# Attention denominators by way of HBM instead of 0/1 products on TensorE

## The reference

```
x = x + attention(layernorm(x))     # 16 heads of 16 channels, rotary q and k, ALiBi bias, softmax
x = x + layernorm(x) @ (W + C V_r).T + b
```

## Time and profile before

| | |
|---|---|
| median of three runs | 2109.35 us (2106.3 to 2109.4) |
| the profiled execution | span 2108.7 us; no time beyond its span is listed for it |
| PE busy | 2074.9 us, 98% |
| DVE busy | 1855.8 us, 88% |
| ACT busy | 1513.9 us, 72% |
| POOL busy | 1296.4 us, 61% |
| time from one batch to the next | 62.7 us (1038.66 to 1101.38 for the first product of the spread, in the chain that ended last) |
| mean TensorE clock granted | 0.989 of full speed |

### The profile page before, as it was taken

One profiled execution on the slowest core, in us unless ns is written; L12 is line 12 of the kernel. 1 busy time (PEld: TensorE's weight loads), 2 busy tenths in 40 slices (PEclk: granted clock), 3 DMA queues, 4 the chain that ended last, 5 costly groups with the idle time before them and its releaser, 6 DMA issues.

```text
span 2108.7 us, 81949 instructions
## 1 busy us (share of the span) xinstructions
PE 2074.9 (98%) x33596; PEld 1193.3 (57%) x33596; DVE 1855.8 (88%) x5459; ACT 1513.9 (72%) x2562; POOL 1296.4 (61%) x1093
## 2 busy tenths in 40 slices
PE   6999999999999999999999999999999999999998
PEld 3455555555555555555555555555555555555554
DVE  7899998988998998999898999998999999999972
ACT  2377777777777777787777777777777777777664
POOL 6357566667565667666666666666766666766512
PEclk8699999999999999999999999999999999999999
DMA  5343333433333433334333334334333334333311
GB/s 156 92 115 102 87 112 105 112 116 104 94 103 107 114 113 105 96 101 124 94 113 109 100 97 121 104 105 123 101 86 115 104 109 121 102 95 104 97 51 39
DMA packets 158935, 218.78 MB, mean 104 GB/s; under 512 B 19072, under 2 KB 104960, under 8 KB 158560
## 3 DMA queue, kind: packets, MB, share of 16 engines
q1 hardware_dynamic: 157280, 211.44, 35.5%
q10 hardware_dynamic: 1280, 2.10, 0.3%
HBM read 36.52 MB, written 16.78 MB: 25 GB/s over the span
## 4 chain that ended last, share of the span: by engine, by line
PE 91%; DVE 1%; ACT 1%; issue 1%; POOL 0%; DVEq 0%
PE ps_s L436 30%; PE ps_o L459 21%; PE ps_misc L413 18%; PE ps_misc L400 12%; PE ps_misc L387 3%; PE ps_misc L478 3%; PE ps_t L446 2%; PE ps_misc L469 2%; DVE junk L648 1%; ACT pt L840 0%; PE ps_t L519 0%; ACT x_res L788 0%; ACT x_res L783 0%; DVE x_hat L684 0%; DVE x_res L633 0%
## 5 line engine op out<-in xcount | busy, mean ns | idle before, releaser
L648 DVE CUSTOM_DVE_ANT_0 junk<-ps_s,alibi 128x512 bf16<-128x512 f32 x2004 | 1302.7, 687 | 185.7 <-PE ps_s L436 153.6
L840 ACT ACTIVATE pt<-ps_t 128x1024 f32<-128x1024 f32 x1024 | 1049.6, 1025 | 450.5 <-DVE ps_t L661 441.4
L446 PE MATMUL ps_t<-at 64*128 64x512 f32 x2048 | 762.2, 451 | 2.3 <-ACT pt L840 2.0
L436 PE MATMUL ps_s<-at 64*128 64x512 f32 x2004 | 757.7, 454 | 3.6 <-DVE row_max L648 2.8
L459 PE MATMUL ps_o<-pt,v_one 128*17 128x128 f32 x16384 | 637.4, 273 | 1.4 <-ACT pt L840 1.3
L459 PEld LDWEIGHTS ps_o<-pt,v_one 128*17 128x17 f32 x16384 | 441.1, 98 | 184.2 <-issue 46.0
L436 PEld LDWEIGHTS ps_s<-at 64*128 64x128 f32 x2004 | 325.6, 184 | 240.9 <-DVE row_max L648 133.4
L661 DVE TENSOR_TENSOR ps_t<-ps_t,diag 128x256 f32<-128x256 f32 x1024 | 435.5, 425 | 14.5 <-PE ps_t L446 14.4
L1006 POOL TENSOR_TENSOR rope_b<-raw,rope_sin 128x512 f32<-128x512 f32 x128 | 164.5, 1285 | 327.3 <-ACT raw L820 323.6
L1022 POOL TENSOR_TENSOR halves<-rope_a,swapped 128x512 fp32r<-128x512 f32 x126 | 159.3, 1287 | 322.8 <-DMA swapped<-rope_b 322.8
L446 PEld LDWEIGHTS ps_t<-at 64*128 64x128 f32 x2048 | 328.1, 184 | 13.9 <-ACT pt L840 8.7
(11 more groups left out here) (105 smaller groups left out, 1801.0 us busy)
## 6 DMA issues: line engine op xcount, KB each, us to landing
at<-halves SPq DMA_DIRECT2D x192, 512.0 KB, 4.0
swapped<-rope_b SPq DMA_DIRECT2D x256, 128.0 KB, 2.6
x_in<-in_L_attn_x_dram SPq DMA_DIRECT2D x32, 512.0 KB, 5.2
num<-o_sb SPq DMA_DIRECT2D x512, 32.0 KB
x_res<-in_L_attn_x_dram SPq DMA_DIRECT2D x32, 512.0 KB, 4.3
out_dram<-x_hat SPq DMA_DIRECT2D x32, 512.0 KB, 5.8
at<-spread_den SPq DMA_DIRECT2D x60, 64.0 KB
at<-max_t ACTq DMA_DIRECT2D x128, 16.0 KB
```

Of the source, the lines that this page charges most:

```text
L436: pe.matmul(scores_bank(n, t), operand(n, 0)[:, t * P:(t + 1) * P], operand(n, 1), start=True, stop=True).then_inc(s_done, 1)
L446: pe.matmul(ps_t[:, j, :], operand(n, 1)[:, j * P:(j + 1) * P], operand(n, 0), start=True, stop=True).then_inc(t_done, 1)
L648: dve.tensor_tensor_reduce(unused, scores_bank(n, t), alibi[:, off:off + N], 1.0, LOWEST, ALU.add, ALU.max, row_max[:, hb % 2, t, hh:hh + ...
L840: act.activation(pt[:, h % 2, 2 * pair:2 * pair + 2, :], ps_t[:, 2 * pair:2 * pair + 2, :], ACT.Exp).then_inc(exp_done, 1)
```

## The change

The denominators of a batch are written to an array in HBM (`den_dram`) instead of the tile. At slot 29 SP waits for the four writes and loads them back as 128 rows of 64. DVE takes one reciprocal of 128 x 64 in half-slot 32 b + 59. At slot 30 SP waits for it and writes the result to HBM (`recip_dram`). At slot 31 SP waits for that write and issues four loads that repeat each head's row over 16 partitions, into the new tile `spread`. DVE multiplies `spread` by `num` in half-slots 64 and 65, one later than before. The 64 products of a batch on PE and their table are gone. The zeros for `clear_max` move from the table's free rows to free rows of the tile that holds the turned maxima.

```diff
-XT, DEN, X2T = (-26, -25), (63, 64), (79, 80)
+XT, X2T = (-26, -25), (79, 80)
+GATHER_SLOT, RECIPROCAL_SLOT, PARK_SLOT, SPREAD_SLOT = 29, 29, 30, 31
+DIVIDE = (64, 65)
...
-        den = sb("den", [P, P])
+        den = sb("den", [P, HALF])
+        spread = sb("spread", [P, KC, N])
...
+        den_dram = nc.dram_tensor("den_dram", (NB, H, N), F32).ap()
+        recip_dram = nc.dram_tensor("recip_dram", (NB, H, N), F32).ap()
...
-            def denominators(b, half):
-
-                if half == 0:
-                    dve.wait_ge(den_placed, 16 * G * (b + 1))
-                mine = slice(half * HALF, (half + 1) * HALF)
-                dve.reciprocal(den[0:T * H, mine], den[0:T * H, mine]).then_inc(den_done, 1)
+            def denominators(b):
+
+                dve.wait_ge(den_gathered, 16 * (b + 1))
+                dve.reciprocal(den[:, :], den[:, :]).then_inc(den_done, 1)
...
             def divide(b, kc):
-                dve.wait_ge(misc_full, full_at["den", b, kc])
                 if kc == 0:
                     dve.wait_ge(num_placed, 16 * T * G * (b + 1))
+                    dve.wait_ge(spread_placed, 16 * G * (b + 1))
                     if b:
                         dve.wait_ge(x1_done, 2 * b)
-                dve.tensor_tensor(attn_t[:, kc, :], bank_at("den", b, kc), num[:, kc, :], ALU.mult).then_inc(attn_done, 1)
+                dve.tensor_tensor(attn_t[:, kc, :], spread[:, kc, :], num[:, kc, :], ALU.mult).then_inc(attn_done, 1)
...
+            def gather_denominators(b):
+
+                sp.wait_ge(den_placed, 16 * G * (b + 1))
+                if b:
+                    sp.wait_ge(recip_parked, 16 * b)
+                sp.dma_start(den[:, :], den_dram[b].rearrange("h (t q) -> (h t) q", q=HALF)).then_inc(den_gathered, 16)
+
+            def park_reciprocals(b):
+
+                sp.wait_ge(den_done, b + 1)
+                sp.dma_start(recip_dram[b].rearrange("h (t q) -> (h t) q", q=HALF), den[:, :]).then_inc(recip_parked, 16)
+
+            def spread_denominators(b):
+
+                sp.wait_ge(recip_parked, 16 * (b + 1))
+                if b:
+                    sp.wait_ge(attn_done, KC * b)
+                for g in range(G):
+                    src = recip_dram[b, HG * g:HG * (g + 1), :].rearrange("(o i) q -> o i q", o=1).broadcast_to([D, HG, N])
+                    sp.dma_start(spread[(g % 2) * HALF:(g % 2 + 1) * HALF, g // 2, :], src).then_inc(spread_placed, 16)
...
-                    sp.dma_start(den[g * T * HG:(g + 1) * T * HG, :], o_sb[D::32, :, :]).then_inc(den_placed, 16)
+                    dst = den_dram[b, HG * g:HG * (g + 1), :].rearrange("i (t q) -> t i q", t=T)
+                    sp.dma_start(dst, o_sb[D::32, :, :]).then_inc(den_placed, 16)
```

More of the change, by code:

```diff
@@ L98, in shape_constants @@
     of_head = of_head.reshape(P, -1)
[L101 to L108, removed]
+    return {"rope_cos": rows(cos, cos), "rope_sin": rows(sin, -sin), "before": before, "diag": diag,
             "qpat": np.concatenate([qpat, qpat], 0), "kpat": spread(kpat).astype(f), "pick": np.concatenate([spread(pick), of_head], 1).astype(f), "ident": np.eye(P, dtype=f)}
@@ L161, in layer @@
         max2 = sb("max2", [P, T, 2 * 8])
-        max_t = sb("max_t", [2 * 8, N], F32R)
+        turned = sb("turned", [P, N], F32R)
+        max_t = turned[0:2 * 8, :]
+        no_max = turned[HALF:HALF + M_ROWS, :].bitcast(F32)
         junk = sb("junk", [P, 2, N], mybir.dt.bfloat16)
@@ L289, in bank_of @@
                 return "misc"
-            return {"den": "s0", "proj": "s1", "x2t": "s0", "ffn": "s1"}.get(kind, "misc")
+            return {"proj": "s1", "x2t": "s0", "ffn": "s1"}.get(kind, "misc")
         def bank_at(kind, b, u):
@@ L470, in max_rows @@
                 misc_filled(ins, ("max", hb), max_turned, hb + 1)
[L472 to L481, removed]
             def turn_weights():
@@ L576, in tensor_program @@
                             turn_tokens("x2t", b, kc, x_hat2, xhat_done2, b + 1 + (b == NB - 1), x2t_done)
-                        b, quarters = due(now, DEN[kc])
-                        if b is not None:
-                            spread_denominators(b, kc)
                     if hb is not None and half == 1:
@@ L685, in add_linear @@
                                   other[:, two, :], ALU.add).then_inc(done, 1)
-            dve.memset(spread_den[T * H:P, :, :, :], 0.0)
-            dve.memset(den[T * H:P, :], 0.0)
+            dve.memset(no_max, 0.0)
             dve.memset(alibi[:, 0:U_W // 2], 0.0).then_inc(cleared, 1)
@@ L735, in vector_program @@
                         slope_block(2 * (n - 3) + half)
-                    for part in range(2):
-                        b = batch_at(slot, (29, 30)[part])
-                        if b is not None and half == 1 - part:
-                            denominators(b, part)
+                    b = batch_at(slot, RECIPROCAL_SLOT)
+                    if b is not None and half == 1:
+                        denominators(b)
                     now = 2 * slot + half
                     for kc in range(KC):
-                        b = complete_at(now, DEN[kc])
+                        b = complete_at(now, DIVIDE[kc])
                         if b is not None:
@@ L1109, in sync_program @@
                                      o_sb[32 * t:32 * t + D, :, :]).then_inc(num_placed, 16)
+                b = batch_at(slot, GATHER_SLOT)
+                if b is not None:
+                    gather_denominators(b)
+                b = batch_at(slot, PARK_SLOT)
+                if b is not None:
+                    park_reciprocals(b)
+                b = batch_at(slot, SPREAD_SLOT)
+                if b is not None:
+                    spread_denominators(b)
                 hb = half_at(slot, -8)
```

4 lines of the change are left out of this document (1 added, 3 removed).

## The result

The changed kernel takes **2336.26 us** in the median of four runs (2329.26 to 2346.06), against 2109.18 of the kernel before beside it: a ratio of 1.108 (1.105 to 1.112). The forecast was 2227, with a range that ended at 2300. The direction and the stall came out, but the kernel lost 227 us where 118 were forecast. The profiled execution has a span of 2339.0 us and a mean clock of 0.947, where before had 2108.7 and 0.989.

The account below looks back on a forecast made before the run. PE (98% busy) was taken to bound the kernel, DVE (88%) next. Stall less gain, 31 x (4.5 - 1.05) = 107, plus 11 for the last batch, made 118 us on 2108.7: 2227, range 2155 to 2300.

Parts of the forecast that it names:

- the stall: Half-slots 60 to 61: PE waits for row maxima held up behind DVE's wait for the gather, 4.5 us a batch.
- DVE's wait: At the reciprocal in half-slot 59: the gather lands at 1037.0, 5.3 us after DVE's arrival.
- rival (0.17): PE's clock falls at each stall, one to two half-slots at half speed: 59 us more, 2286; chance 0.17.
- the gap of the earlier trace: Start of the run before: clock at 0.51 after 4 us with PE busy for 0.16; 4.5 us called hardly more.
- the prediction's own sign of being wrong: Listed as showing the forecast wrong: PE's clock below 1 behind the stalls.
- The division reads both operands from SBUF; I cost this at nothing: Divisions in half-slots 64 and 65: no cost for two SBUF operands; ten per cent either way would be 4 us.
- The gain: Half-slots 61 to 66 without the spread products on PE: 1.05 us a batch, not the full 1.8.
- the estimate after it: Start of half-slot 61 to half-slot 67 after the change: 8.35 + 2.65 = 11.0 us, where it was 12.1.
- DVE becomes the limit from half-slot 62 on: Without the products DVE sets the pace: 1.55 us a half-slot without extras, 2.15 with a division.
- The second chain: Reciprocal, park, spreads, division: hidden behind the row maxima of half-slots 60 to 64 with 1.4 us to spare.
- The rival that had it late: Reciprocal-to-division chain late as well: 31 x 1.6 = 50 us more, 2277; chance 0.12.
- The tail: Last batch, nothing to hide behind: projection 7 us later, slow clock +4, 11 us in all, between 7 and 17.

Follow-up runs that it names:

- the swap in the queue: Changed kernel with the gather issued at slot 28 instead of 29, ahead of the two 512 KB transfers: 2199.44 us, 1.042 of before.
- no chain and no hold: Changed kernel without gather, park and spread (output not normalised), GpSimd's subtraction waiting until both divisions are done: 2100.26 us, 0.997 of before.
- the kernel with no chain: Changed kernel without gather, park and spread, reciprocal and division working on ones, output not normalised: 2166.24 us, 1.026 of before.

## Why the prediction was wrong

**The stall was right in place and size.** 4.5 us a batch were forecast, and 59-60 rose by 4.36. The gather stands behind the two big transfers and moves when their data has; the packets and the swap in the queue show it. That agrees with the Trainium skill's rule in the prediction (DMA: Bandwidth & Descriptors, Queues, rings and completion order). DVE's wait was 4.8 us in the mean for a forecast of 5.3.

**The step that failed: the clock was kept as a rival (0.17) and not in the forecast.** My argument was that PE keeps working until just before, and that 4.5 us is hardly more than the gap of the earlier trace rows. That gap was the only row I had, and the clock *had* fallen behind it. With the stall taken as certain, the row spoke for the rival. The clock fell in 27 of 27 batches, behind gaps of PE of 2.9 to 5.6 us, and with that the prediction's own sign of being wrong was there (a clock below 1 behind the stalls). Its price was right: 1.9 forecast, 2.09 measured, 65 us in all. The Trainium skill's passage named there (TensorE: Matmul & The Clock Gate, HAM oscillation) agrees with this: 0.50 of the clock behind the stall of every batch.

**"The division reads both operands from SBUF; I cost this at nothing"** also failed. The operation isn't slower by itself (0.69 us), so the range I gave of ten per cent looked at the wrong thing. It is now shut out while GpSimd does its 1.89 us subtraction, where the same operation with a PSUM operand wasn't beside a GpSimd product of 1.28 us; the Trainium skill's section quoted above says so in advance. This is 1.01 us a batch, 31 us. I had read DVE, PE and SP side by side, and not GpSimd.

**The gain was 0.24 us a batch (0.26 as what is left of after's 7.20) and not 1.05**, another 25 us. It was the only term that I took from a single batch, and that one was slow: 1034.02 to 1046.13 is 12.11 us, where the same stretch takes 3.46 + 4.36 + 3.95 = 11.77 in the mean. That is 0.34 of the error. Another 0.26 is in the estimate after it, 11.05 for a stretch that takes 3.45 + 3.73 + 4.13 = 11.31 with no chain and no hold: "DVE becomes the limit from half-slot 62 on" was one half-slot early, and I let its 1.55 us hold for 61 and 62 too, which take 1.68 and 1.77 at PE's own pace. The last 0.2 is the rest of the batch, 0.26 longer in that kernel (47.09 for 46.83) by half-slot 79, less 0.05 in 59-60.

**The second chain was hidden, as forecast.** Park and spread landed in 1.45 and 2.66 us in the median, where 1.8 and 2.6 had been assumed, and the division never waited for them but in the last batch. The rival that had it late did not come true in after. In the kernels with another order of the queue it did.

**The tail was right.** From the issue of the last denominators to the projection it took 2316.87 - 2303.90 = 12.97 us, against 2089.04 - 2083.03 = 6.01: 7.0 later, as forecast. PE stood still for 10.06 us. From there to the end it takes 22.1 instead of 19.7, so 2.5 for the clock where I had 4: 9.4 for 11. The chain that ended last, in after:

```profile
2307.09 1.78 DMA den<-den_dram
2309.47 1.45 DMA recip_dram<-den
...
2312.79 2.55 DMA spread<-recip_dram
...
2316.87 3.64 PE ps_misc L411 x32
```

**The sum again.** Forecast: 31 x (4.5 - 1.05) + 11 = 118. Measured: 31 x (4.36 + 2.09 + 1.01 - 0.26) + 9.4 = 233, where the spans differ by 230. Between the two sums lie 115: 65 are the clock, 31 the held division and 25 the gain, less 4 for the stall and 2 for the tail. With the rival's clock in it, the forecast would have been 2286, still 50 us short by the two other terms.

## What to carry to other kernels

A small transfer that an engine waits for is priced by what stands ahead of it in its queue, and each cheap swap there names another victim, so look at all readers of the queue together. Where a forecast contains a stall of PE of some 3 us or more, the fall of the clock belongs in the sum, and one of 1.4 us already belongs among the rivals. When an operand moves from PSUM to SBUF, lay GpSimd's time line beside VectorE's, and take a gain from the mean over many batches, with the next engine's own pace as its limit.

## What the runs showed of the hardware

- Stalls of PE of 2.9 to 5.6 us dropped the granted clock to 0.50 in 27 of 27 batches of after, and it stayed there for about 7 us in 18 of them and 3.4 in 9, although PE was busy through most of that. It cost some 2 us only, as DVE was nearly the limit anyway. Gaps of 1.3 to 2.4 us were sometimes enough: it fell in 16 of 27 batches behind waits of 1.35 to 1.84 us in the kernel with no chain, and that cost 1.4 us each time.
- A VectorE product of two SBUF tiles takes 0.69 us alone, and up to 2.42 beside a GpSimd operation of 1.89 us on 128x1024 tiles: in after it ended 0.55 us behind that one, whenever it had begun (0.89 to 1.93 us). GpSimd's next one went from 1.89 to 2.22. With one operand in PSUM it took 0.69 beside a GpSimd product of 128x512 (30 times), and with two in SBUF 0.69 beside a GpSimd power of 128x4 (9 times).
- The park of 32 KB into HBM landed 1.45 us after its issue in an empty queue, and 2.0 to 4.7 us after it (median 3.1) behind two transfers of 512 KB. The gather of 32 KB from HBM took 1.8 to 1.9 us with nothing before it, and 2.9 to 5.4 (median 3.6) behind them.
